# Layer 3 attention on one core: both casts of the probabilities on ScalarE, the low half of the values on VectorE

## The chip, the core and the metric

The kernel runs on one core of a Trainium2 chip (trn2). The metric is the device time of one execution in microseconds. The engines are PE (TensorE), DVE (VectorE), ACT (ScalarE), POOL (GpSimd) and SP (SyncE, which here only issues DMAs). Each has its own queue, works it off in order, and is tied to the others by semaphores alone.

## What is computed

The reference takes x (16 batches x 56 tokens x 128) through four pairs of cross attention and feed-forward, with ctx_1024 (16 x 1500 x 128) as keys and values. Layer 3's attention, the part that is changed, is plain multi-head attention with 16 heads of 8 columns, a bias on every projection and a key mask:

```python
q = (q_input @ W_Q + b_Q); k = (kv_input @ W_K + b_K); v = (kv_input @ W_V + b_V)   # 16 heads x 8
sim = jnp.einsum('bhqd,bhkd->bhqk', q, k) / jnp.sqrt(jnp.float32(D_H))
sim = jnp.where(mask, neg_inf, sim)
attn = jax.nn.softmax(sim, axis=-1)
out = jnp.einsum('bhqk,bhkd->bhqd', attn, v)
return out @ W_O + b_O
```

x then gets this sum and goes through a mixture of eight experts (`l3f`), the last stage.

## The kernel before

Layer 3's attention is `small_head_attention`: `attend_sets` (stage `l3att`) makes the outputs of all heads, `join_sets` (`l3comb`) applies W_O. The 16 heads are four sets of four. One step of `attend_sets` starts one set of one batch: 224 rows (4 heads x 56 tokens) against 1500 keys, which are 12 chunks of 125. 64 steps, batch by batch, run in a loop unrolled eight times. u is the step within the unrolled body and g = u % 4 the set. Work of three sets overlaps: in step n PE makes the scores of set n, the transposed scores of set n-1 and the output of set n-2. The loops call `one(n, u, known)` on each engine, and the order of the work is written out by hand there.

Numbers that need more than TensorE's fast format (fp32r) are split into a rounded high part and a low part, the rest. The kernel does it for queries, keys, values, maxima and probabilities. One fp32r matmul works on each part. A plain fp32 matmul is shown in the trace as two instructions of the slow kind.

PSUM has eight banks of 512 columns. Banks 0 to 2 take the scores of half a set (`rows`, 112 x 1500), bank 2 also the projection of keys for the next batch and the denominators; banks 3 to 5 the transposed scores (`turned`, two parts of six chunks), bank 5 also the projection of values; banks 6 and 7 the outputs and the transposed maxima.

The steps around the change, by engine, with the lines of the code of before:

- PE (L1949 to L2063), in this order: `values` for chunks 0 to 3 (waits for the first low part of the probabilities and for the low values); `maxima`, two transposes of the negated maxima (L2000, waits `negs_in`); `rows(0)` (L1971); `turned(0)` (L1990, waits for the copied maxima, `m_in`, and, ahead of the two chunks in bank 5, until the values in that bank have been read); `values` for chunks 4, 5 and 11; `rows(1)`; `turned(1)`; `values` for chunks 6 to 10; then the projections of keys (L1914, g < 3), denominators (L2055, g = 3) and values (L1920, all g but 1).
- ACT (L2101 to L2141): exponentials of the first part (`powers(0)`, L2110), cast of its chunks 0 to 4 into PH (`high_part`, L2116), exponentials of the second part, copy of the output (L2124), high part of the keys (L2069), high part of the values into VS (L2079), and a plain copy of the values to VF (L2081), which waits until POOL is done with VF.
- POOL (L2192 to L2209): low values VF - VS (`low_values`, L2169), block queries of the next batch (L2178), and then the low parts of the probabilities, PL = P - PH, two instructions of 5 chunks (1120 elements), each as soon as its cast is there (`ph_in`, L2208).
- DVE (L2251 to L2289): low keys (L2220), on g = 0 the reciprocal of the denominators (L2257), copy of the transposed maxima into QB (L2262), maximum of the first half of the rows (L2266), on g = 0 the division of an output (L2272), maximum of the second half (L2275), cast of the two maxima to fp32r (L2280), their low part (L2282, signals `negs_in`), and at last the cast of the second part of the probabilities (L2289, the one that POOL's second L2208 waits for).

`SPLIT` is 5: of the six chunks of each part the first five are split into PH and PL, the sixth is multiplied in fp32 (L2024). WOS holds W_O for `join_sets`; POOL clears it at the start (`cleared`), and SP fills it by eight DMAs (L1900), after the first remap of the keys and before the third context load.

In the expert stage `l3f`, POOL splits weights (L583, L585) and adds a bias (L596), while DVE works through a layer norm whose reciprocal root is made by `rsqrt`. Two of its lines:

```python
chain(v.tensor_tensor(y2, out, out, ALU.mult))     # L142
chain(v.tensor_tensor(tt, y2, half, ALU.mult))     # L143
```

Of the kernel before, what the change touches and what calls it, by code (L numbers as in the profile page):

```python
# [11 lines left out]
ALU = mybir.AluOpType  # L12
# [28 lines left out]
PART = CHUNKS // 2  # L41
SPLIT = PART - 1
HIDDEN = -2.0 ** 126
# [125 lines left out]
class Kernel(Stack):  # L169
# [1597 lines left out]
    def small_head_attention(self):  # L1767


        t = self.t  # L1770
        self.stage = "l3"
        with ExitStack() as whole:
            OC = self.sb(whole, "OC", [SETS * VCOLS, BATCH, SETS, TOK])
            cout = self.sb(whole, "cout", [128, 1])
            WOS = self.sb(whole, "WOS", [SETS * VCOLS, SETS, D])
            wos_in = self.sem(whole, "wos_in")
            self.attend_sets(OC, cout, WOS, wos_in)
            self.join_sets(OC, cout, WOS)

    def attend_sets(self, OC, cout, WOS, wos_in):  # L1780
# [10 lines left out]
        with ExitStack() as ctx:  # L1791
# [6 lines left out]
            cT = [self.sb(ctx, f"cT{s}", [128, KEYS]) for s in range(2)]  # L1798
            VF = self.sb(ctx, "VF", [CHUNK, 64, 8])
            SEL = self.sb(ctx, "SEL", [ROWS17, SETS, VCOLS])  # L1800
# [21 lines left out]
            P = [self.sb(ctx, f"P{s}", [CHUNK, CHUNKS, SET_ROWS]) for s in range(2)]  # L1822
            PH, PL = ([self.sb(ctx, f"{n}{s}", [CHUNK, 2, SPLIT, SET_ROWS], F32R) for s in range(2)]
                      for n in ("PH", "PL"))
# [5 lines left out]
                 "maskb_in"))  # L1830
            (k_ps, kh_in, kl_in, v_ps, vh_in, vf_in, vl_in, den_ps, inv_in, on_in, qb_in, sr_ps, top_in, nh_in, negs_in, t_ps, m_in,
             st_ps, p_in, ph_in, pl_in, o_ps, o_in) = (self.sem(ctx, n) for n in (
                 "k_ps", "kh_in", "kl_in", "v_ps", "vh_in", "vf_in", "vl_in", "den_ps", "inv_in", "on_in", "qb_in", "sr_ps", "top_in", "nh_in",
                 "negs_in", "t_ps", "m_in", "st_ps", "p_in", "ph_in", "pl_in", "o_ps", "o_in"))
# [11 lines left out]
            def _(sp):  # L1846
# [47 lines left out]
                for b in range(BATCH):  # L1894
                    if b == 0:
                        sp.wait_ge(cleared, 1)
                        for h in range(SETS):
                            for r in range(2):
                                at = VCOLS * h + 8 * r
                                sp.dma_start(WOS[at:at + 8, :, :], t["L3_xattn_W_O"].rearrange(  # L1900
                                    "(g h j) d -> h j g d", g=SETS, h=SETS)[h]).then_inc(wos_in, 16)
                    else:
                        extract(b - 1)
                    if b + 2 < BATCH:
                        sp.wait_ge(v_ps, BANKS * (b + 1))
# [19 lines left out]
            def _(pe):  # L1925
# [23 lines left out]
                def one(n, u, known):  # L1949
# [27 lines left out]
                    def turned(part):  # L1977
# [7 lines left out]
                        for k in range(PART):  # L1985
                            if k == 4 and part == 0 and g != 1 and (
                                    known is None or known - 1 < GROUPS - (SETS if g else 0)):
                                pe.wait_ge(vf_in, thirds)
                            at = CHUNK * (PART * part + k)
# [14 lines left out]
                    def values(chunks):  # L2004
# [11 lines left out]
                        for k in chunks:  # L2016
                            first, last = k == 0, k == CHUNKS - 2
                            if k % PART < SPLIT:
                                pe.matmul(out, VS[s][:, k, g, :], PH[u % 2][:, k // PART, k % PART, :],  # L2019
                                          start=first, stop=False)  # L2020
                                mm = pe.matmul(out, VS[s][:, k, g, :], PL[u % 2][:, k // PART, k % PART, :],  # L2021
                                               start=False, stop=last)
# [52 lines left out]
            def values_out(act, b, s, i, bank):  # L2075
# [3 lines left out]
                act.copy(heads(s, i)[:, :, 0:8], src).then_inc(vh_in, 1)  # L2079
                act.wait_ge(vl_in, b * BANKS + i)  # L2080
                act.copy(VF[:, :, :], src).then_inc(vf_in, 1)  # L2081

            @block.scalar
            def _(act):
# [16 lines left out]
                def one(n, u, known):  # L2101
# [11 lines left out]

                    def high_part():
                        act.wait_ge(p_in, 2 * n - 1)
                        act.copy(PH[s][:, 0, :, :], P[s][:, 0:SPLIT, :]).then_inc(ph_in, 1)  # L2116

# [9 lines left out]
                    if live(known, 1, GROUPS):  # L2127
                        powers(0)
                        high_part()
                        powers(1)  # L2130
                    if live(known, 2, GROUPS):
                        outputs()
# [14 lines left out]
            def _(g):  # L2147
# [5 lines left out]
                chain(g.memset(negs[:, :, :, :].bitcast(F32), 1.0))  # L2153
                chain(g.memset(WOS[:, :, :], 0.0))
                chain(g.memset(SEL[:, :, :], 0.0))
# [10 lines left out]

                def low_values(b, s, i):
                    g.wait_ge(vf_in, b * BANKS + i + 1)
                    g.tensor_tensor(heads(s, i)[:, :, 8:16], VF[:, :, :], heads(s, i)[:, :, 0:8], ALU.subtract  # L2169
                                    ).then_inc(vl_in, 1)  # L2170

                def low_queries(n):
# [9 lines left out]

                for i in range(BANKS):
                    low_values(0, 0, i)
                g.wait_ge(vl_in, BANKS)
                for n in range(2 * SETS):
                    low_queries(n)
                g.wait_ge(q3_in, 2 * SETS)
                for x in range(SETS):
                    block_queries(0, 0, x)  # L2190

                def one(n, u, known):  # L2192
                    b, x = n // SETS, u % SETS
                    if x == 3 and live(known, 1, GROUPS - SETS):
                        low_values(b + 1, 1 - u // SETS, 0)
                    if x == 0 and live(known, 1, GROUPS - SETS):
                        low_values(b, u // SETS, 1)
                    if x == 1 and (known is None or SETS < known < GROUPS):
                        low_values(b, u // SETS, 2)
                    if known is None or known < GROUPS - SETS:  # L2200
# [3 lines left out]
                    if live(known, 1, GROUPS):  # L2204
                        s = (u - 1) % 2
                        for part in range(2):
                            g.wait_ge(ph_in, 2 * n - 1 + part)
                            g.tensor_tensor(PL[s][:, part, :, :], P[s][:, PART * part:PART * part + SPLIT, :],  # L2208
                                            PH[s][:, part, :, :], ALU.subtract).then_inc(pl_in, 1)  # L2209

# [3 lines left out]
            def _(v):  # L2214
                chain = Chain(v, step)

                def low_keys(b, i, bank):
                    at = slice(BANK_KEYS * i, BANK_KEYS * i + BANK_KEYS)
                    v.wait_ge(kh_in, b * BANKS + i + 1)
                    v.scalar_tensor_tensor(out=kl[:, at], in0=PS[:, bank, 0:BANK_KEYS], scalar=bk[:, 0:1],  # L2220
                                           in1=kh[:, at], op0=ALU.add, op1=ALU.subtract).then_inc(kl_in, 1)

                layer_norm(v, chain, XN, X, ln, 1e-5, xn_ready)
# [23 lines left out]
                for n in range(2 * SETS):  # L2247
                    scaled(n)
                v.wait_ge(cleared, 1)

                def one(n, u, known):  # L2251
# [3 lines left out]
                    if g == 0 and live(known, 8, GROUPS):  # L2255
                        v.wait_ge(den_ps, (n - SETS) // SETS)
                        v.reciprocal(inv[:, :, :].rearrange("p g q -> p (g q)"), PS[0:ROWS17, 2, 0:SET_ROWS]  # L2257
                                     ).then_inc(inv_in, 1)
                    if live(known, 1, GROUPS):
                        a = (u - 1) % UNROLL  # L2260
                        v.wait_ge(t_ps, n)
                        v.tensor_copy(QB[a // SETS][96:99, a % SETS, :],  # L2262
                                      PS[0:3, 6 + a % 2, 256:256 + SET_ROWS]).then_inc(m_in, 1)
                    if live(known, 0, GROUPS):
                        v.wait_ge(sr_ps, 2 * n + 1)
# [7 lines left out]
                    if live(known, 0, GROUPS):  # L2273
# [10 lines left out]
                    if live(known, 1, GROUPS):  # L2284
                        s = (u - 1) % 2
                        v.wait_ge(p_in, 2 * n)
                        if known is None or known >= 3:
                            v.wait_ge(o_ps, n - 2)
# [3 lines left out]
                v.wait_ge(on_in, BATCH)  # L2292

# [131 lines left out]
```

## Time and profile before

| | |
|---|---|
| median of 3 runs | 1998.93 us (1997.3 to 2000.82) |
| profiled execution | 1990.49 us, its span 1988.8 us |
| granted TensorE clock over the span | 0.909 of full speed |
| PE, DVE, ACT, POOL busy | 1638.5, 1367.2, 929.6, 701.4 us |

The profile is one execution. It names each instruction by engine, line and tiles, gives its start and duration, and says for idle time which instruction ended it. An instruction that waits for a semaphore counts as idle until it starts; a wait after its start is part of its duration. Matmuls overlap, so the duration of one (0.27 us for 224 columns) is longer than the distance to the next. The loop of `l3att` runs from about 1280 to 1825 us, the experts from about 1850 us to the end.

### The profile page before, as it was taken

How to read it: one execution, taken by the hardware profiler on the slowest of the kernel's cores; microseconds unless marked ns; L12 is line 12 of the kernel's file. 1: busy time of each engine (PE TensorE's matmuls, PEld its weight loads, DVE VectorE, ACT ScalarE, POOL GpSimd, SP SyncE). 2: the span in 40 equal slices, each digit the busy share in tenths (PEclk: the TensorE clock that was granted, in tenths of full speed). 3: DMA queues.
4: the chain of work that ended last, by engine and by line, in shares of the span. 5: the costliest groups of instructions: out<-in, count | busy, mean ns of one | idle time of the engine just before them, and what ended most of it. 6: DMA issues, size and time to landing. Idle time of an engine off the chain costs nothing. (4 is left out here: it accounts for less than half of the span.)

```text
span 1988.8 us, 30871 instructions
## 1 busy us (share of the span) xinstructions
PE 1638.5 (82%) x10566; PEld 1375.8 (69%) x10566; DVE 1367.2 (69%) x2269; ACT 929.6 (47%) x1342; POOL 701.4 (35%) x607
## 2 busy tenths in 40 slices
PE   3994546433899999999999994599999999996796
PEld 2994334313789999999999972277777777774695
DVE  5214523465588888888888843578888888884498
ACT  1432211120466666666666622366666666663331
POOL 1110000000034323333332300378787878774231
PEclk8997878765799999999999997799999999998798
DMA  2113254003111111111011000424343434340110
GB/s 52 33 32 119 92 168 147 2 0 94 44 32 46 49 31 31 52 40 31 31 59 34 0 3 3 107 69 107 87 104 87 104 87 104 87 89 3 54 43 20
DMA packets 97952, 118.10 MB, mean 59 GB/s; under 512 B 16641, under 2 KB 82722, under 8 KB 97890
## 3 DMA queue, kind: packets, MB, share of 16 engines
q1 hardware_dynamic: 97890, 117.32, 22.5%
q8 instruction: 34, 0.56, 0.1%
q14 instruction: 28, 0.23, 0.0%
HBM read 78.51 MB, written 0.46 MB: 40 GB/s over the span
## 5 line engine op out<-in xcount | busy, mean ns | idle before, releaser
L2208 POOL TENSOR_TENSOR l3att_PL<-l3att_P,l3att_PH 125x1120 fp32r<-125x1120 f32 x128 | 330.1, 2579 | 122.1 <-DVE l3att_PH L2289 61.3
L1605 ACT CAST l2att_PT<-PS 125x512 fp32r<-125x512 f32 x336 | 175.5, 594 | 221.4 <-PE PS L1540 221.4
L1670 DVE TENSOR_REDUCE l2att_neg<-PS 128x1 f32<-128x1500 f32 x112 | 192.7, 1721 | 75.2 <-PE PS L1533 75.1
L2110 ACT ACTIVATE l3att_P<-PS 125x1344 f32<-125x1344 f32 x128 | 165.5, 1293 | 137.4 <-PE PS L1990 135.4
L1676 DVE TENSOR_TENSOR l2att_PT<-PS,l2att_PT 125x512 fp32r<-125x512 f32 x336 | 210.4, 681 | 2.0 <-ACT l2att_PT L1605 2.0
L1496 POOL CAST l_QH<-l_QP 128x128 fp32r (+1 forms) x112 | 54.2, 484 | 390.0 <-POOLq L1285 228.5
L1540 PEld LDWEIGHTS PS<-all_ident,l2att_P 128*125 128x125 f32 x1344 | 164.8, 189 | 14.5 <-DVE l2att_P L1684 6.0
L1614 ACT ACTIVATE l2att_P<-PS,l2att_neg 128x1500 f32<-128x1500 f32 x112 | 171.2, 1528 | 5.2 <-DVE l2att_neg L1670 5.2
L1572 PE MATMUL PS<-l2att_PT,l2att_cc 125*128 125x256 f32 x576 | 170.6, 296 | 0.0
L1540 PE MATMUL PS<-all_ident,l2att_P 128*125 128x128 f32 x1344 | 166.5, 274 | 4.5 <-DVE l2att_P L1684 4.5
L1574 PE MATMUL PS<-l2att_PT,l2att_cc 125*128 125x256 f32 x576 | 162.9, 283 | 0.0
L1576 PE MATMUL PS<-l2att_PT,l2att_cc 125*128 125x256 f32 x576 | 162.8, 283 | 0.0
L2019 PE MATMUL PS<-l3att_PH,l3att_VS 125*68 125x224 f32 x640 | 148.9, 274 | 12.9 <-POOL l3att_PL L2208 12.7
L2275 DVE TENSOR_REDUCE l3att_negm<-PS 112x1 f32<-112x1500 f32 x64 | 110.2, 1721 | 62.0 <-PE PS L1971 62.0
L2021 PE MATMUL PS<-l3att_PL,l3att_VS 125*68 125x224 f32 x640 | 144.0, 266 | 0.0
L1971 PE MATMUL PS<-l3att_KS,l3att_QB 97*112 97x500 f32 x384 | 125.0, 428 | 19.4 <-DVE l3att_inv L2257 7.7
L1531 PE MATMUL PS<-l2att_cTh,l_QH 128*128 128x500 f32 x336 | 133.4, 397 | 5.8 <-DVE l2att_cTl L1698 4.5
L1532 PE MATMUL PS<-l2att_cTl,l_QH 128*128 128x500 f32 x336 | 131.7, 392 | 0.0
L1533 PE MATMUL PS<-l2att_cTh,l_QL 128*128 128x500 f32 x336 | 131.1, 390 | 0.0
L1684 DVE TENSOR_SCALAR l2att_P<-l2att_P,l2att_inv 128x1500 f32<-128x1500 f32 x112 | 121.3, 1083 | 3.9
L2266 DVE TENSOR_REDUCE l3att_negm<-PS 112x1 f32<-112x1500 f32 x64 | 110.1, 1721 | 19.1 <-PE PS L1971 19.1
L1990 PEld LDWEIGHTS PS<-l3att_QB,l3att_KS 99*125 99x125 f32 x768 | 100.0, 190 | 23.3 <-DVE l3att_QB L2262 16.2
(510 smaller groups left out, 3755.6 us busy)
## 6 DMA issues: line engine op xcount, KB each, us to landing
l3att_KS<-l3att_kh SPq DMA_DIRECT2D x128, 187.5 KB, 4.0
l_cT<-in_ctxT SPq DMA_DIRECT2D x8, 1500.0 KB, 26.0
l_c<-in_ctx SPq DMA_DIRECT2D x8, 1500.0 KB
l_cT<-in_ctxT SPq DMA_DIRECT2D x16, 750.0 KB
l_c<-in_ctx SPq DMA_DIRECT2D x16, 750.0 KB
l3att_cT<-in_ctxT SPq DMA_DIRECT2D x16, 750.0 KB, 4.8
l3att_KS<-l3att_kl SPq DMA_DIRECT2D x64, 187.5 KB, 3.8
l0f_w<-in_L_ffn_W SPq DMA_DIRECT2D x16, 256.0 KB, 3.1
```

The lines of the kernel that those rows point to most:

```text
L1540: mm = pe.transpose(PS[0:CHUNK, 3 * s1 + g, 128 * j:128 * j + 128], P[s1][:, at:at + CHUNK], ident[:, :])
L1572: pe.matmul(out2, cc[:, slot, k, 0, :], PT[:, k, two, 0, :], start=first, stop=False)
L1574: pe.matmul(out2, cc[:, slot, k, 1, :], PT[:, k, two, 0, :], start=False, stop=False)
L1576: mm = pe.matmul(out2, cc[:, slot, k, 0, :], PT[:, k, two, 1, :], start=False, stop=last)
L1605: act.copy(PT[:, 4 * g:4 * g + 4, PLACE[u1], 0, :], PS[0:CHUNK, 3 * s1 + g, :].rearrange("k (c r) -> k c r", r=128)).then_inc(hi_in, 1)
L1614: act.activation(Pv, Pv if padded else PS[:, 3 * s:3 * s + 3, 0:BANK_KEYS], ACT.Exp, bias=neg[:, s:s + 1], accum_out=total[:, s:s + 1]).th ...
L1670: v.tensor_reduce(neg[:, s:s + 1], E, XY_AXES, ALU.max, negate=True).then_inc(top_in, 1)
L1676: v.tensor_tensor(PT[:, 4 * g:4 * g + 4, at, 1, :], PS[0:CHUNK, 3 * s1 + g, :].rearrange("k (c r) -> k c r", r=128), PT[:, 4 * g:4 * g + 4 ...
L2019: pe.matmul(out, VS[s][:, k, g, :], PH[u % 2][:, k // PART, k % PART, :], start=first, stop=False)
L2021: mm = pe.matmul(out, VS[s][:, k, g, :], PL[u % 2][:, k // PART, k % PART, :], start=False, stop=last)
L2110: act.activation(P[s][:, PART * part:PART * part + PART, :].rearrange("p (i j) r -> p i (j r)", j=2), PS[0:CHUNK, 3:6, 0:2 * SET_ROWS], AC ...
L2208: g.tensor_tensor(PL[s][:, part, :, :], P[s][:, PART * part:PART * part + SPLIT, :], PH[s][:, part, :, :], ALU.subtract).then_inc(pl_in, 1)
```

## The change

ScalarE makes both casts of the probabilities. PH and PL hold eleven chunks in a row: chunk 5 is now split as well, and only chunk 11 is left in fp32. ACT's `high_part(0)` and POOL's first subtraction cover six chunks (1344 elements), the second of each five (1120). DVE's cast L2289 is gone. The low values are made by DVE from the PSUM bank itself, behind the copy of the maxima and ahead of the first maximum of the step; ACT's copy to VF, the tile VF and POOL's subtraction are gone, and PE's wait ahead of bank 5 in `turned(0)` is on DVE's result. DVE's cast of the two maxima becomes a max of the tile with itself. The reciprocal waits for the division of the batch before. WOS lies in XN, and POOL clears it after its first block queries (`wos_clear`, for which SP waits).

```diff
-SPLIT = PART - 1
+HALVED = CHUNKS - 1
-            WOS = self.sb(whole, "WOS", [SETS * VCOLS, SETS, D])
+            WOS = self.XN[0:SETS * VCOLS, 0:SETS, :]
# PE
                             if k == 4 and part == 0 and g != 1 and (
                                     known is None or known - 1 < GROUPS - (SETS if g else 0)):
-                                pe.wait_ge(vf_in, thirds)
+                                pe.wait_ge(vl_in, thirds)
-                            if k % PART < SPLIT:
+                            if k < HALVED:
# SP
-                        sp.wait_ge(cleared, 1)
+                        sp.wait_ge(wos_clear, 1)
# ACT
                 act.copy(heads(s, i)[:, :, 0:8], src).then_inc(vh_in, 1)
-                act.wait_ge(vl_in, b * BANKS + i)
-                act.copy(VF[:, :, :], src).then_inc(vf_in, 1)
-                    def high_part():
-                        act.wait_ge(p_in, 2 * n - 1)
-                        act.copy(PH[s][:, 0, :, :], P[s][:, 0:SPLIT, :]).then_inc(ph_in, 1)
+                    def high_part(part):
+                        some = slice(PART * part, min(PART * part + PART, HALVED))
+                        act.wait_ge(p_in, 2 * n - 1 + part)
+                        act.copy(PH[s][:, some, :], P[s][:, some, :]).then_inc(ph_in, 1)
                         powers(0)
-                        high_part()
+                        high_part(0)
                         powers(1)
+                        high_part(1)
# POOL
-                chain(g.memset(WOS[:, :, :], 0.0))
-                for i in range(BANKS):
-                    low_values(0, 0, i)
-                g.wait_ge(vl_in, BANKS)
+                g.wait_ge(xt_ps, 2)
+                g.memset(WOS, 0.0).then_inc(wos_clear, 1)
-                    if x == 3 and live(known, 1, GROUPS - SETS):
-                        low_values(b + 1, 1 - u // SETS, 0)
...
-                            g.tensor_tensor(PL[s][:, part, :, :], P[s][:, PART * part:PART * part + SPLIT, :],
-                                            PH[s][:, part, :, :], ALU.subtract).then_inc(pl_in, 1)
+                            some = slice(PART * part, min(PART * part + PART, HALVED))
+                            g.tensor_tensor(PL[s][:, some, :], P[s][:, some, :], PH[s][:, some, :],
+                                            ALU.subtract).then_inc(pl_in, 1)
# DVE
+                def low_values(b, s, i, bank):
+                    v.wait_ge(vh_in, b * BANKS + i + 1)
+                    v.tensor_tensor(heads(s, i)[:, :, 8:16], PS[0:CHUNK, bank, :].rearrange("p (x j) -> p x j", j=8),
+                                    heads(s, i)[:, :, 0:8], ALU.subtract).then_inc(vl_in, 1)
                     scaled(n)
+                    if n < BANKS:
+                        low_values(0, 0, n, 3 + n)
+                v.sem_inc(on_in, 1)
                         v.wait_ge(den_ps, (n - SETS) // SETS)
+                        v.wait_ge(on_in, (n - SETS) // SETS)
                                       PS[0:3, 6 + a % 2, 256:256 + SET_ROWS]).then_inc(m_in, 1)
+                    if g == 3 and live(known, 1, GROUPS - SETS):
+                        low_values(b + 1, 1 - u // SETS, 0, 5)
+                    if g == 0 and live(known, 1, GROUPS - SETS):
+                        low_values(b, u // SETS, 1, 5)
+                    if g == 1 and (known is None or SETS < known < GROUPS):
+                        low_values(b, u // SETS, 2, 5)
-                        v.tensor_copy(negs[:, u % 2, :, 1], negm[:, u % 2, :]).then_inc(nh_in, 1)
+                        v.tensor_tensor(negs[:, u % 2, :, 1], negm[:, u % 2, :], negm[:, u % 2, :], ALU.max
+                                        ).then_inc(nh_in, 1)
-                        v.tensor_copy(PH[s][:, 1, :, :], P[s][:, PART:PART + SPLIT, :]).then_inc(ph_in, 1)
```

## Rows read from the trace of the kernel before

**Rows 1.** The page, its first part: busy time, share, instructions of each engine.
```profile
PE 1638.5 (82%) x10566; PEld 1375.8 (69%) x10566; DVE 1367.2 (69%) x2269; ACT 929.6 (47%) x1342; POOL 701.4 (35%) x607
```
**Rows 2.** Two stretches: length, then PE, PEld, DVE, ACT, POOL busy, clock, DMA, GB/s.
```profile
1340.00:1780.00 440.00, 415.39 (x2770) 322.07 (x2767) 371.23 (x386) 280.57 (x333) 351.67 (x200) 1.00 0.42 96
1802.00:1820.00 18.00, 11.81 (x84) 9.29 (x84) 12.22 (x13) 8.12 (x10) 11.43 (x5) 1.00 0.00 1
```
**Rows 3.** Timeline of one step: start, duration (us), engine, line, operation, tiles [idle before].
```profile
1361.92 2.56 POOL L2208 TENSOR_TENSOR l3att_PL<-l3att_P,l3att_PH 125x1120 fp32r<-125x1120 f32 x1 [0.20 <-ACT l3att_PH L2116]
...
1363.14 1.36 DVE L2280 CAST l3att_negs<-l3att_negm 112x2 fp32r<-112x2 f32 x1
...
1364.54 0.16 DVE L2282 TENSOR_TENSOR l3att_negs<-l3att_negm,l3att_negs 112x2 fp32r<-112x2 f32 x1
...
1364.61 0.32 PE L2019 MATMUL PS<-l3att_PH,l3att_VS 125*68 125x224 f32 x1 [0.34 <-POOL l3att_PL L2208]
...
1364.62 0.74 DVE L2289 CAST l3att_PH<-l3att_P 125x1120 fp32r<-125x1120 f32 x1
...
1365.28 0.73 DVE L2220 SCALAR_TENSOR_TENSOR l3att_kl<-PS,l3att_bk,l3att_kh 128x500 fp32r<-128x500 f32 x1
...
1365.49 0.35 PE L2000 MATMUL PS<-all_ident,l3att_negs 112*3 112x112 f32 x2
...
1366.04 0.38 DVE L2262 CAST l3att_QB<-PS 3x224 fp32r<-3x224 f32 x1
...
1366.48 0.92 PE L1990 MATMUL PS<-l3att_QB,l3att_KS 99*125 99x224 f32 x6
...
1366.59 1.72 DVE L2266 TENSOR_REDUCE l3att_negm<-PS 112x1 f32<-112x1500 f32 x1 [0.16 <-PE PS L1971]
...
1367.43 1.29 ACT L2110 ACTIVATE l3att_P<-PS 125x1344 f32<-125x1344 f32 x1 [2.44 <-PE PS L1990]
...
1368.36 0.93 PE L1971 MATMUL PS<-l3att_KS,l3att_QB 97*112 97x500 f32 x3
...
1368.75 1.13 ACT L2116 CAST l3att_PH<-l3att_P 125x1120 fp32r<-125x1120 f32 x1
...
1369.13 0.82 PE L1990 MATMUL PS<-l3att_QB,l3att_KS 99*125 99x224 f32 x6
...
1369.96 2.57 POOL L2208 TENSOR_TENSOR l3att_PL<-l3att_P,l3att_PH 125x1120 fp32r<-125x1120 f32 x1 [1.41 <-ACT l3att_PH L2116]
```
**Rows 4.** By tile negs: count, shortest/median/longest ns, first and last start (us).
```profile
L2280 DVE CAST l3att_negs<-l3att_negm x64: 170/1378/1484, 1286.0 to 1809.9; 112x2 fp32r<-112x2 f32 x64
L2282 DVE TENSOR_TENSOR l3att_negs<-l3att_negm,l3att_negs x64: 161/163/165, 1286.2 to 1811.3; 112x2 fp32r<-112x2 f32 x64
```
**Rows 5.** Timeline in the experts, POOL then DVE; last, line L142 by source.
```profile
1899.57 1.28 POOL L585 TENSOR_TENSOR l3f_w1l<-l3f_w,l3f_w1h 128x512 fp32r<-128x512 f32 x1
1900.81 2.35 POOL L596 TENSOR_TENSOR l3f_XB<-all_XN,l3f_b 128x1024 f32<-128x1024 f32 x1
...
1899.76 1.12 DVE L142 TENSOR_TENSOR l3f_nwork<-l3f_rstd 128x8 f32<-128x8 f32 x1
1900.91 2.28 DVE L143 TENSOR_TENSOR l3f_nwork<-l3f_nwork 128x8 f32<-128x8 f32 x1
...
L142 DVE TENSOR_TENSOR l3f_nwork<-l3f_rstd x27: 166/167/1116, 1852.4 to 1978.7; 128x8 f32<-128x8 f32 x27
```
**Rows 6.** Groups by line, 1340 to 1780 us: count | busy us, mean ns | idle before.
```profile
L2208 POOL TENSOR_TENSOR l3att_PL<-l3att_P,l3att_PH 125x1120 fp32r<-125x1120 f32 x107 | 276.0, 2580 | 89.1 <-DVE l3att_PH L2289 52.0 <-ACT l3att_PH L2116 37.1
...
L2169 POOL TENSOR_TENSOR l3att_VS<-l3att_VF,l3att_VS 125x512 fp32r<-125x512 f32 x40 | 50.0, 1251 | 0.0
L2024 PE MATMUL PS<-l3att_P,l3att_VS 125*68 125x224 f32 x212 | 48.7, 352 | 0.0
...
L2220 DVE SCALAR_TENSOR_TENSOR l3att_kl<-PS,l3att_bk,l3att_kh 128x500 fp32r<-128x500 f32 x40 | 29.3, 732 | 0.0
L2257 DVE RECIPROCAL l3att_inv<-PS 68x224 f32<-68x224 f32 x14 | 21.7, 1547 | 0.0
```

More of the change, by code:

```diff
@@ L1798, in attend_sets @@
             cT = [self.sb(ctx, f"cT{s}", [128, KEYS]) for s in range(2)]
-            VF = self.sb(ctx, "VF", [CHUNK, 64, 8])
             SEL = self.sb(ctx, "SEL", [ROWS17, SETS, VCOLS])
@@ L1822, in attend_sets @@
             P = [self.sb(ctx, f"P{s}", [CHUNK, CHUNKS, SET_ROWS]) for s in range(2)]
-            PH, PL = ([self.sb(ctx, f"{n}{s}", [CHUNK, 2, SPLIT, SET_ROWS], F32R) for s in range(2)]
+            PH, PL = ([self.sb(ctx, f"{n}{s}", [CHUNK, HALVED, SET_ROWS], F32R) for s in range(2)]
                       for n in ("PH", "PL"))
@@ L1830, in attend_sets @@
                  "maskb_in"))
-            (k_ps, kh_in, kl_in, v_ps, vh_in, vf_in, vl_in, den_ps, inv_in, on_in, qb_in, sr_ps, top_in, nh_in, negs_in, t_ps, m_in,
+            (k_ps, kh_in, kl_in, v_ps, vh_in, vl_in, wos_clear, den_ps, inv_in, on_in, qb_in, sr_ps, top_in, nh_in, negs_in, t_ps, m_in,
              st_ps, p_in, ph_in, pl_in, o_ps, o_in) = (self.sem(ctx, n) for n in (
-                 "k_ps", "kh_in", "kl_in", "v_ps", "vh_in", "vf_in", "vl_in", "den_ps", "inv_in", "on_in", "qb_in", "sr_ps", "top_in", "nh_in",
+                 "k_ps", "kh_in", "kl_in", "v_ps", "vh_in", "vl_in", "wos_clear", "den_ps", "inv_in", "on_in", "qb_in", "sr_ps", "top_in", "nh_in",
                  "negs_in", "t_ps", "m_in", "st_ps", "p_in", "ph_in", "pl_in", "o_ps", "o_in"))
@@ L2017, in values @@
                             first, last = k == 0, k == CHUNKS - 2
-                            if k % PART < SPLIT:
-                                pe.matmul(out, VS[s][:, k, g, :], PH[u % 2][:, k // PART, k % PART, :],
+                            if k < HALVED:
+                                pe.matmul(out, VS[s][:, k, g, :], PH[u % 2][:, k, :],
                                           start=first, stop=False)
-                                mm = pe.matmul(out, VS[s][:, k, g, :], PL[u % 2][:, k // PART, k % PART, :],
+                                mm = pe.matmul(out, VS[s][:, k, g, :], PL[u % 2][:, k, :],
                                                start=False, stop=last)
@@ L2165, in _ @@
                 g.sem_inc(cleared, 1)
[L2167 to L2170, printed above, removed]
                 def low_queries(n):
@@ L2190, in _ @@
                     block_queries(0, 0, x)
+                g.wait_ge(xt_ps, 2)
+                g.memset(WOS, 0.0).then_inc(wos_clear, 1)
                 def one(n, u, known):
                     b, x = n // SETS, u % SETS
-                    if x == 3 and live(known, 1, GROUPS - SETS):
-                        low_values(b + 1, 1 - u // SETS, 0)
[L2196 to L2199, printed above, removed]
                     if known is None or known < GROUPS - SETS:
@@ L2283, in one @@
                                         ALU.subtract).then_inc(negs_in, 1)
[L2284 to L2288, printed above, removed]
-                        v.tensor_copy(PH[s][:, 1, :, :], P[s][:, PART:PART + SPLIT, :]).then_inc(ph_in, 1)
                 run_steps(v, GROUPS, LAG, UNROLL, one, peeled=1)
-                v.wait_ge(on_in, BATCH)
+                v.wait_ge(on_in, BATCH + 1)
     def join_sets(self, OC, cout, WOS):
```

## The prediction

> **What bounds the kernel now.** The change lies in layer 3's attention alone, so I read the timings of that stage and leave the rest at its present time. The busy table [rows 1] gives PE 82% of the span and DVE 69%. The table of stretches [rows 2] says more: from 1340 to 1780 us PE is busy 415.39 of 440 us at a granted clock of 1.00, DVE 371.23, POOL 351.67, ACT 280.57. So PE is nearly full, and an edit that only lightens DVE can win little. The subtract of L2282, once a step, starts from 1286.2 to 1811.3 us [rows 4]: 63 steps take 525.1 us, 8.33 us each.
>
> The timeline of one step [rows 3] is to be read as a ring. POOL makes the low half of the probabilities (L2208, first part, "PL0") from 1361.92 to 1364.48. PE stood idle 0.34 us for it and starts the value matmuls at 1364.61 (L2019, "V4"); then come the transposes of the maxima (L2000, 1365.49), DVE's copy of them (L2262, ends 1366.42), the first transposed scores (L1990, end 1367.40), ACT's exponential (L2110, 1367.43), ACT's cast (L2116, 1368.75 to 1369.88), and PL0 again at 1369.96. That is 8.04 us round. A second ring runs beside it: reduce (L2266), rows (L1971), reduce (L2275), keys, V4, transposes, rows. They are close to each other.
>
> The third thing to see is the cast of L2280. It moves 2 elements and takes 1.36 us in that step, 1378 ns in the median and 170 ns at the least [rows 3, 4]. It starts at 1363.14 and ends at 1364.50, 0.02 us after POOL's PL0. So DVE waited for POOL's instruction. L2282, behind it, reads two SBUF tiles and takes 163 ns, but no POOL instruction ran then: the second POOL subtract (PL1) waits for DVE's own cast L2289.
>
> **Does the new max escape this wait?** The change replaces the cast by a max of `negm` with itself, and hands the cast that kept POOL quiet (L2289) to ACT. In the trace of before there is a twin of both instructions, in the expert layer's square root [rows 5]. L142 is a tensor_tensor of one tile with itself, 8 elements, and L143 a tensor_tensor of two tiles, 8 elements. Undisturbed L142 takes 0.17 us. With POOL's L585 running (to 1900.85) it takes 1.12 us and ends at 1900.88. POOL's next instruction L596 starts at once, and L143, issued at 1900.91, takes 2.28 us and ends at 1903.19, 0.03 us after L596. So a tensor_tensor with both inputs in SBUF waits as the cast does, and between two dependent DVE instructions POOL's queued instruction gets in.
> The Trainium skill has a rule against this change: "SBUF — State Buffer", section "SBUF: two separate sides", says that a DVE instruction with two SBUF inputs and a GpSimd instruction that reads SBUF exclude each other for a whole instruction. [rows 5] agree. The page "VectorE: DVE Perf Modes", section "Why `tensor_tensor` can't do 2×_2P or 4×", taken alone, would let the fp32 max keep clear of the two-port mode and so of the wait, which would give the second rival's time below; [rows 5] speak against that reading.
>
> **The new step, term by term.** Let H0 and H1 be ACT's casts, P0 and P1 its exponentials, P0 starting at 0.
> H0 starts at 1.32 [rows 3]. It grows from 1120 to 1344 elements: 1.13 by proportion is 1.36, by the slope between cast and exponential (1.29 - 1.13 for 224 elements) 1.29; I take 1.33. It ends at 2.65. PL0 starts 0.08 later, as in [rows 3]. Its slope is (2580 - 1251) / (1120 - 512) = 2.19 ns per element [rows 6], so 1344 elements take 3.07: it ends at 5.80.
> P1 starts when the second half of the transposed scores is there: 1.77 from DVE's first reduce to PE's rows (L1971), 0.77 to L1990, 0.82 for it [rows 3]; that reduce starts some 0.45 ahead of P0, right behind the low values, so P1 starts at about 2.9. Then 1.29 and 1.13: H1 ends at about 5.4, before PL0. So PL1 stands ready and follows PL0 at once, 2.56 more (5 chunks, as now), to 8.36.
> DVE's second reduce follows the rows (0.93) and ends at -0.45 + 1.77 + 0.97 + 1.72 = 4.0, so the max waits 1.8 us for PL0 and ends at 5.83; the subtract waits for PL1 and ends at 8.39.
> Behind the subtract, on DVE, stand the low keys, the copy of the maxima and now the low values, and PE's transposed scores wait for both of the latter. From the subtract's end: low keys 0.66 (0.73 less the overlap of 0.07 with the instruction ahead, 1365.36 to 1365.28), copy 0.41, low values 0.66, then the last two matmuls of L1990 with the hops on either side 0.48 (0.39 of the 0.92 for six, 0.06 and 0.03) = 2.21. The transposes need 0.44 from the subtract to the copy and hide behind the low keys. The low values read a bank and one SBUF tile like L2220, whose 732 ns for 500 elements [rows 6] I take for 512; that kind overlapped PL1 undisturbed at 0.73 [rows 3]. The same subtraction on POOL takes 1.25 (L2169), the upper bound; 0.68 for 512 contiguous elements is about the lower.
> One turn: 8.39 + 2.21 = 10.60. Where no low values are made (one step in four) 1.01 follows the copy directly (1366.42 to 1367.43): 8.39 + 0.66 + 0.41 + 1.01 = 10.47. Where the reciprocal (1.55, [rows 6]) stands for the low keys: 11.42. Four steps: 2 x 10.60 + 10.47 + 11.42 = 43.09, 10.77 a step. The last three have neither low keys nor low values: 8.39 + 0.84 (transposes 0.36, copy 0.38, hops 0.10) + 1.01 = 10.24.
> 60 x 10.77 + 3 x 10.24 = 676.9, less 525.1 = +151.8. At the end PL1 no longer waits for DVE's last cast: -0.6.
>
> **What is at nothing.** The eleventh split chunk replaces one fp32 chunk (two L2024 of 352 ns, [rows 6]) by two matmuls like L2019, at most 0.32 each [rows 3]: PE gains 0.06 to 0.2 a step, but it lies under DVE's 1.72 us reduce. ACT loses the copy to VF and gains H1, and POOL loses 1.25 in three of four steps; both have room (ACT about 6.4 of 10.8). The wait on `on_in` ahead of the reciprocal is a batch old. WOS is now cleared behind POOL's first block queries; SP waits for that ahead of its eight DMAs (L1900), and behind them stand the third context load and the second batch's remap, which waits for low keys made only in the first steps of the loop anyway. The start-up on POOL gets shorter by up to 3 us; I take 0 and keep -3 to +3.
>
> Sum: +151.2 us. The profiled execution took 1990.49 (span 1988.8), the median is 1998.93; 1990.49 becomes 2141.7 and the median 2150.1: **2150 us**.
>
> **Rivals.**
> 1. One wait only: H1 comes too late for PL1 to be queued, the subtract slips in behind the max. The margin is 5.80 - 5.4 = 0.4 us, which is thin. Then the first ring decides: PL0's end, 0.13, V4 0.88, transposes and copy 0.78, low values 0.66, 0.48, P0 to PL0's end 5.80 = 8.73; without low values 8.60; with the reciprocal 9.07; four steps 35.13, against 33.3. 60 x 8.78 + 3 x 8.60 - 525.1 - 0.6 = +27: 2026 us.
> 2. The max and subtract don't wait at all (the fp32 rule above): the same ring, since PL0 has grown by 0.49 and H0 by 0.20 and PE already stood waiting for PL0 in [rows 3]. About 2024. Either way slower, for the same reason.
> 3. Faster: DVE's queue is what bounds, and PL0 lands in time for V4. DVE would lose 1.21 (cast) and 0.74 (L2289) and gain 0.55 a step, and PE's idle would go: (440 - 415.39) / 53 steps = 0.46 a step [rows 2], with 0.2 of the split chunk 0.66, x 63 = -42 at the most: 1957. It decides from the point at which H0 and PL0 together are over before PE reaches V4; they are already 0.34 late in [rows 3] and grow by 0.69.
> 4. The forecast, and TensorE's clock falls besides. Of four steps PE would be busy 0.944 x 33.3 - 0.8 = 30.6 of 43.1 us, 71%. For it: no stretch of this stage was so thin for long. Against: from 1802 to 1820 it was busy 11.81 of 18 us, 66%, at 1.00 [rows 2]. If a fifth of the steps ran at 1.2 GHz, PE's 7.7 us a step would be some 15: 12 x 4 = +48, 2200.
>
> **Chances.** Forecast 0.74, one wait or none (1 and 2) 0.13, clock 0.08, faster or no change (3) 0.05. The forecast's own bounds: low values at 1.25, 0.52 x 45 = +23; hops and overlaps, some eight a turn, read from one step, 0.4 a turn either way, 25. With half of case 4 and a margin below, since the 0.4 us of rival 1 can fail in some steps only: 2100 to 2205. This kernel's timing tells changes from about 0.2%, 4 us. Faster 0.04, same 0.02, slower 0.94.
>
> **What would show it.** In the changed profile the max of L2280's place should take about 1.7 to 1.9 us and the subtract of L2282's about 2.5, ending within 0.05 of POOL's two subtracts, which follow each other without a gap. Reduce to reduce should be 10.5 to 11.4. DVE's idle should stay small, PE's idle should move to the transposes, waiting for `negs`. If the subtract takes 0.16 and PE waits for L2208 ahead of V4, rival 1 or 2 holds, and the duration of the max tells which. A clock under 1.00 between 1340 and 1900 us would be rival 4.

## The result

The changed kernel takes 2123.78 us (median of 4 runs, 2119.01 to 2130.65), the kernel before 1999.47 us: the ratio is 1.0625, 95% interval 1.059 to 1.0661. The profiled execution took 2119.01 us with a span of 2117.3. The forecast was 2150, its range 2100 to 2205.

The page of the changed kernel, its busy table, answers to [rows 1]:

```profile
span 2117.3 us, 30746 instructions
...
PE 1696.6 (80%) x10566; PEld 1414.1 (67%) x10566; DVE 1450.6 (69%) x2253; ACT 983.9 (46%) x1358; POOL 671.1 (32%) x559
```

DVE has 16 instructions fewer and is busy 83 us longer. Where that sits is in the instructions that touch the tile `negs`, the answer to [rows 4] (count, shortest, median and longest ns, first and last start; below, who waited for the subtract):

```profile
L2282 DVE TENSOR_TENSOR l3att_negs<-l3att_negm x64: 161/1934/2146, 1290.1 to 1934.3; 112x2 fp32r<-112x2 f32 x64
L2285 DVE TENSOR_TENSOR l3att_negs<-l3att_negm,l3att_negs x64: 161/2480/2495, 1290.3 to 1936.4; 112x2 fp32r<-112x2 f32 x64
...
who waited for it (us, times):
  PE PS L1999: 50.7, 34
```

The max takes 1934 ns in the median, the subtract behind it 2480; each handles two elements per partition and takes 0.16 us undisturbed. The subtract starts from 1290.3 to 1936.4 us: 63 steps in 646.1 us, 121.0 more than in [rows 4]. The two profiled executions are 128.5 us apart; of the other 7.5, 4.1 lie ahead of the first subtract and 3.4 behind the last.

But PE waited for the subtract 34 times, not 63. The timeline of two steps that follow each other, in the answer to [rows 3], shows both kinds (start, duration, engine, line; in brackets the idle time ahead):

```profile
1503.75 5.56 POOL L2195 TENSOR_TENSOR l3att_PL<-l3att_P,l3att_PH 125x1344 fp32r<-125x1344 f32 x2 [2.91 <-ACT l3att_PH L2114]
...
1504.86 1.94 DVE L2282 TENSOR_TENSOR l3att_negs<-l3att_negm 112x2 fp32r<-112x2 f32 x1
...
1505.08 1.13 ACT L2114 CAST l3att_PH<-l3att_P 125x1120 fp32r<-125x1120 f32 x1
...
1506.84 2.49 DVE L2285 TENSOR_TENSOR l3att_negs<-l3att_negm,l3att_negs 112x2 fp32r<-112x2 f32 x1
1506.91 0.32 PE L2018 MATMUL PS<-l3att_PH,l3att_VS 125*68 125x224 f32 x1 [0.93 <-POOL l3att_PL L2195]
...
1509.47 0.35 PE L1999 MATMUL PS<-all_ident,l3att_negs 112*3 112x112 f32 x2 [1.52 <-DVE l3att_negs L2285]
...
1512.58 1.59 PE L1970 MATMUL PS<-l3att_KS,l3att_QB 97*112 97x500 f32 x3
...
1513.97 1.24 PE L1989 MATMUL PS<-l3att_QB,l3att_KS 99*125 99x224 f32 x6
...
1514.17 3.07 POOL L2195 TENSOR_TENSOR l3att_PL<-l3att_P,l3att_PH 125x1344 fp32r<-125x1344 f32 x1 [4.34 <-ACT l3att_PH L2114]
...
1515.97 1.29 DVE L2282 TENSOR_TENSOR l3att_negs<-l3att_negm 112x2 fp32r<-112x2 f32 x1
...
1516.57 1.13 ACT L2114 CAST l3att_PH<-l3att_P 125x1120 fp32r<-125x1120 f32 x1
...
1517.29 0.16 DVE L2285 TENSOR_TENSOR l3att_negs<-l3att_negm,l3att_negs 112x2 fp32r<-112x2 f32 x1
...
1517.78 2.60 POOL L2195 TENSOR_TENSOR l3att_PL<-l3att_P,l3att_PH 125x1120 fp32r<-125x1120 f32 x1 [0.54 <-ACT l3att_PH L2114]
```

In the first step the second cast ends at 1506.21, before POOL's first subtraction (1503.75 + 3.07 = 1506.82). POOL's two subtractions run as one block to 1509.31 (the row with x2). The max ends with the first of them, at 1506.80, and the subtract ends with the block, at 1509.33. PE stood still for 0.93 and 1.52 us. In the second step PE is slow: the rows take 1.59 us where they took 0.93, the second transposed scores 1.24 against 0.82 [rows 3]. So ACT's second cast ends at 1517.70, 0.46 after the first subtraction, POOL's second subtraction isn't running yet, and the subtract passes in 0.16 us. The slow PE accounts for all of it: from the start of the rows to the end of the second transposed scores it is 1.57 us in the first step and 2.63 in the second, 1.06 more, and the second cast, counted from the start of the exponential, ends 1.06 us later (6.24 against 5.18).

The two steps as stretches (from reduce to reduce; length, then PE, PEld, DVE, ACT, POOL busy, granted clock, DMA, GB/s), against [rows 2]:

```profile
1500.38:1510.81 10.43, 7.43 (x45) 5.16 (x45) 8.89 (x8) 5.85 (x6) 6.54 (x4) 1.00 0.06 9
1510.81:1520.34 9.53, 9.53 (x58) 7.58 (x56) 6.62 (x7) 6.36 (x7) 5.63 (x3) 0.82 0.30 97
```

The long step has a clock of 1.00 and leaves PE idle for 3 of 10.43 us. The next has 0.82: the granted clock is 0.50 (1.2 GHz) from 1512 to 1514 us and 1.00 again from 1515. PE is busy all through, and the step is 0.9 us shorter. From step 11 on (counted from 0, at 1397.5 us) long and short steps alternate to the end. The long ones are in turn one without low values, like the one shown, and one with the reciprocal and low values (11.49 us, also at 1.00, PE busy for 8.54).

### The profile page after: what moved, and what is told of

It is laid out like the page before. It is cut to its first block and busy times, and to the rows that moved or that the text cites. A ratio compares the mean times of both kernels' runs of the same rounds, so it can differ in the third digit from the quotient of the medians.

```text
span 2117.3 us, 30746 instructions
## 1 busy us (share of the span) xinstructions
PE 1696.6 (80%) x10566; PEld 1414.1 (67%) x10566; DVE 1450.6 (69%) x2253; ACT 983.9 (46%) x1358; POOL 671.1 (32%) x559
## 5 line engine op out<-in xcount | busy, mean ns | idle before, releaser
L2195 POOL TENSOR_TENSOR l3att_PL<-l3att_P,l3att_PH 125x1344 fp32r<-125x1344 f32 (+1 forms) x128 | 359.1, 2818 | 272.6 <-ACT l3att_PH L2114 271.7
L2018 PE MATMUL PS<-l3att_PH,l3att_VS 125*68 125x224 f32 x704 | 168.2, 281 | 27.7 <-POOL l3att_PL L2195 25.6
L2277 DVE TENSOR_REDUCE l3att_negm<-PS 112x1 f32<-112x1500 f32 x64 | 110.1, 1721 | 85.6 <-PE PS L1970 85.6
L1970 PE MATMUL PS<-l3att_KS,l3att_QB 97*112 97x500 f32 x384 | 148.1, 492 | 23.9 <-DVE l3att_negm L2268 14.1
L2020 PE MATMUL PS<-l3att_PL,l3att_VS 125*68 125x224 f32 x704 | 164.8, 275 | 0.0
L2114 ACT CAST l3att_PH<-l3att_P 125x1344 fp32r<-125x1344 f32 (+1 forms) x128 | 156.2, 1220 | 4.0
L1989 PEld LDWEIGHTS PS<-l3att_QB,l3att_KS 99*125 99x125 f32 x768 | 119.0, 214 | 34.1 <-DVE l3att_QB L2258 13.2
L1989 PE MATMUL PS<-l3att_QB,l3att_KS 99*125 99x224 f32 x768 | 133.7, 305 | 2.4 <-DVE l3att_QB L2258 1.3
L2018 PEld LDWEIGHTS PS<-l3att_PH,l3att_VS 125*68 125x68 f32 x704 | 101.6, 144 | 45.0 <-issue 43.9
```

The lines of the kernel that those rows point to most:

```text
L1989: mm = pe.matmul(PS[0:CHUNK, 3 + k // 2, SET_ROWS * (k % 2):SET_ROWS * (k % 2) + SET_ROWS], KS[s][:, g, at:at + CHUNK], QB[s][:, g, :], st ...
L2018: pe.matmul(out, VS[s][:, k, g, :], PH[u % 2][:, k, :], start=first, stop=False)
L2020: mm = pe.matmul(out, VS[s][:, k, g, :], PL[u % 2][:, k, :], start=False, stop=last)
L2195: g.tensor_tensor(PL[s][:, some, :], P[s][:, some, :], PH[s][:, some, :], ALU.subtract).then_inc(pl_in, 1)
```

## The experiments

Four kernels are the changed one with an edit, run together.

**The cast again.** Is it the tensor_tensor?

```diff
-                        v.tensor_tensor(negs[:, u % 2, :, 1], negm[:, u % 2, :], negm[:, u % 2, :], ALU.max
-                                        ).then_inc(nh_in, 1)
+                        v.tensor_copy(negs[:, u % 2, :, 1], negm[:, u % 2, :]).then_inc(nh_in, 1)
```

> The changed kernel with the max of the maxima tile with itself put back to the cast of before. Theory (any DVE instruction that needs the second way into SBUF waits for POOL's whole subtraction): the cast waits as the max does, 1.9 us, the subtract behind it 2.5 us in about half the steps; 2124 us, within 8. Rival (a tensor_tensor is worse than a cast, or better): a difference of more than 0.5% from the changed kernel.

Measured: 2119.96 us, ratio to the kernel before 1.0609 (1.0591 to 1.0627), which overlaps the changed kernel's. The cast's median is 1936 ns, the subtract's 2474, and PE waits for the subtract 34 times. Max and cast are the same to this kernel.

**Three reduces.** The high part, its negative and the low part are each made by an instruction with one SBUF input. `negm` gets a fourth axis, the value and its negated high part (its shape and the index in the two reduces of the rows, also edited, are not shown).

```diff
-                        v.tensor_tensor(negs[:, u % 2, :, 1], negm[:, u % 2, :], negm[:, u % 2, :], ALU.max
-                                        ).then_inc(nh_in, 1)
+                        v.tensor_reduce(negs[:, u % 2, :, 1], negm[:, u % 2, :, 0:1], X_AXIS, ALU.max)
+                        v.tensor_reduce(negm[:, u % 2, :, 1].bitcast(F32R), negm[:, u % 2, :, 0:1], X_AXIS, ALU.max,
+                                        negate=True).then_inc(nh_in, 1)
                         v.wait_ge(nh_in, n + 1)
-                        v.tensor_tensor(negs[:, u % 2, :, 2], negm[:, u % 2, :], negs[:, u % 2, :, 1],
-                                        ALU.subtract).then_inc(negs_in, 1)
+                        with nc.allow_low_precision(reason="two terms"):
+                            v.tensor_reduce(negs[:, u % 2, :, 2], negm[:, u % 2, :, :], X_AXIS, ALU.add
+                                            ).then_inc(negs_in, 1)
```

> The changed kernel, but the high part, its negative and the low part of the maxima are made by three tensor_reduce over SBUF, each with one input. Theory (the two waits of DVE on POOL's subtractions are the loss): none of the three takes over 0.25 us, PE never waits for the low part, and the ring over POOL's first subtraction decides at 8.73 us a step: 2026 us, 2015 to 2045. Rival (the low values on DVE or the longer cast and subtraction on their own are the loss): above 2080 us. Second rival (a reduce from SBUF waits as well): 1.9 us for the first reduce and about 2124 us.

Measured: 2032.67 us, ratio 1.0171 (1.0154 to 1.0188). The tile `negs` and one step's timeline:

```profile
L2282 DVE TENSOR_REDUCE l3att_negs<-l3att_negm x64: 156/156/157, 1292.9 to 1852.0; 112x2 fp32r<-112x2 f32 x64
L2287 DVE TENSOR_REDUCE l3att_negs<-l3att_negm x64: 156/158/160, 1293.2 to 1852.3; 112x2 fp32r<-112x4 f32 x64
```
```profile
1505.41 5.61 POOL L2195 TENSOR_TENSOR l3att_PL<-l3att_P,l3att_PH 125x1344 fp32r<-125x1344 f32 x2 [2.79 <-ACT l3att_PH L2114]
...
1506.55 0.16 DVE L2282 TENSOR_REDUCE l3att_negs<-l3att_negm 112x2 fp32r<-112x2 f32 x1
1506.62 0.14 DVE L2283 TENSOR_REDUCE l3att_negm<-l3att_negm 112x2 fp32r<-112x2 f32 x1
...
1506.80 0.16 DVE L2287 TENSOR_REDUCE l3att_negs<-l3att_negm 112x2 fp32r<-112x4 f32 x1
```

All three run in the middle of POOL's block, and none is longer than 0.16 us in any of 64 steps. That takes 91 us away (2123.8 - 2032.7). A step is 559.1 / 63 = 8.87 us. By kind, from reduce to reduce, it is 8.9 us with low values, 8.5 without and 8.84 with the reciprocal (forecast for this case 8.73, 8.60 and 9.07).

**The second cast back on DVE.** One part of the change undone; the max and the subtract stay.

```diff
                         powers(1)
-                        high_part(1)
# DVE, behind the subtract of the maxima
+                    if live(known, 1, GROUPS):
+                        s = (u - 1) % 2
+                        v.wait_ge(p_in, 2 * n)
+                        if known is None or known >= 3:
+                            v.wait_ge(o_ps, n - 2)
+                        v.tensor_copy(PH[s][:, PART:HALVED, :], P[s][:, PART:HALVED, :]).then_inc(ph_in, 1)
```

> The changed kernel with one part undone: the cast of the second part of the probabilities is DVE's last instruction of the step again. Then POOL's second subtraction can't be queued behind the first. Theory: the max still waits 1.8 us, the subtract takes 0.16 in every step, the clock stays at 1.00, and a step takes 8.8 to 9.0 us: 2030 to 2050 us. Rival (the time is lost to the max's wait, not to the subtract's): above 2090 us.

Measured: 2052.13 us, ratio 1.0271 (1.0254 to 1.0288), 2 us above the stated range.

```profile
L2281 DVE TENSOR_TENSOR l3att_negs<-l3att_negm x64: 161/1943/2130, 1292.1 to 1869.3; 112x2 fp32r<-112x2 f32 x64
L2284 DVE TENSOR_TENSOR l3att_negs<-l3att_negm,l3att_negs x64: 160/162/165, 1292.3 to 1871.4; 112x2 fp32r<-112x2 f32 x64
```

The max takes 1.94 us as in the changed kernel, the subtract never waits, and the clock from 1400 to 1800 us is 1.00. So it is the second wait that costs: with the first alone the kernel is 72 us faster. The first wait is mostly hidden, because PE waits for the same POOL instruction. A step without low values takes 8.50 us here and 8.50 with the reduces, so there the wait costs nothing. The others are 0.1 to 0.3 us longer than with the reduces, and those with the reciprocal 1.0 us; how much of this is the wait and how much DVE's cast, which is back, was not separated. Both together are 19 us.

**PE filled.** Twelve matmuls whose results are thrown away, in front of the transposes.

```diff
+                    if known is None or 2 <= known < GROUPS:
+                        pe.wait_ge(top_in, 2 * n)
+                        for k in range(12):
+                            pe.matmul(PS[0:SETS * VCOLS, k % 2, 0:SET_ROWS], VS[(u - 2) % UNROLL // SETS][:, k % 4, (u - 2) % SETS, :],
+                                      PH[u % 2][:, k % 4, :], start=True, stop=True)
                     if live(known, 1, GROUPS):
                         maxima()
```

> The changed kernel with twelve more matmuls a step on PE (results thrown away) between the value matmuls of chunks 0 to 3 and the transposes, where PE idles for the low part of the maxima. Theory (a step with both waits idles PE, the granted clock falls to half in the next step, PE's second scores and with them ACT's second cast come late, the subtract slips in, and that step is the shorter one): the clock stays at 1.00, the subtract waits in nearly every step, and the kernel gets slower although its TensorE is faster: 2145 to 2170 us. Rival (the clock falls are only a cost): faster than the changed kernel, under 2115 us.

Measured: 2157.87 us, ratio 1.0808 (1.0789 to 1.0828). The tile `negs`, then the stretch from 1400 to 1800 us (length; PE, PEld, DVE, ACT, POOL busy; clock):

```profile
L2290 DVE TENSOR_TENSOR l3att_negs<-l3att_negm,l3att_negs x64: 161/2516/2528, 1290.2 to 1972.5; 112x2 fp32r<-112x2 f32 x64
...
  PE PS L1999: 18.1, 60
```
```profile
1400.00:1800.00 400.00, 352.04 (x2362) 270.71 (x2360) 353.14 (x259) 225.52 (x240) 225.25 (x112) 1.00 0.33 76
```

The clock holds at 1.00, and PE waits for the subtract 60 times instead of 34, for 0.3 us each, since the filling takes up the rest. In these steps the filling ends before the subtract does, so it adds nothing: with the reciprocal they take 11.51 us, and 11.48 in the changed kernel. The kernel with the faster TensorE is 34 us slower than the changed one. So the slow spells did open the gap through which the subtract slips. The forecast, made for a clock of 1.00, was 2150 for this case.

**What is left once the waits are gone.** The kernel with the reduces is still 34 us above the kernel before. Two terms were separated; both kernels that follow keep the three reduces.

Ten split chunks instead of eleven, so that the first cast and the first subtraction have 1120 elements (PE multiplies chunk 5 in fp32 again):

```diff
-                            if k < HALVED:
+                            if k < HALVED and k != PART - 1:
# the same line in ACT's cast and in POOL's subtraction
-                        some = slice(PART * part, min(PART * part + PART, HALVED))
+                        some = slice(PART * part, PART * part + PART - 1)
```

> The three reduces, with chunk 5 in fp32 again, so that ACT's first cast and POOL's first subtraction have 1120 elements as before. Theory (without the waits on POOL the ring over POOL's first subtraction decides, and its length counts in full): the step falls from 8.85 us by 0.49 + 0.19 = 0.68 to 8.17, or less where PE becomes the bound: 1990 us, 1984 to 2000. Rival (the kernel with the reduces is bound by something else, such as DVE's low values): above 2015 us.

Measured: 1998.75 us, ratio 1.0011 (0.9998 to 1.0023): 34 us less than with eleven. The sum of the terms, 0.68 x 63, is 43; the next run shows what stands in the way of the rest.

The first subtraction in two instructions, chunks 0 to 3 and 4 to 5:

```diff
-                        for part in range(2):
-                            g.wait_ge(ph_in, 2 * n - 1 + part)
-                            some = slice(PART * part, min(PART * part + PART, HALVED))
+                        for part, first, last in ((0, 0, 4), (0, 4, PART), (1, PART, HALVED)):
+                            if first != 4:
+                                g.wait_ge(ph_in, 2 * n - 1 + part)
+                            some = slice(first, last)
# PE
-                        parts = 1 if chunks[0] < PART else 2
-                        pe.wait_ge(pl_in, 2 * n - 4 + parts)
-                        if parts == 1:
+                        parts = {0: 1, 4: 2, 6: 3}[chunks[0]]
+                        pe.wait_ge(pl_in, 3 * n - 6 + parts)
+                        if parts < 3:
```

> The three reduces and eleven split chunks, but POOL's first subtraction is two instructions, chunks 0 to 3 and 4 to 5, and PE's value matmuls of chunks 0 to 3 wait for the first alone. Theory: the low part of chunks 0 to 3 is there 1.0 us earlier, the ring over POOL's subtraction falls to 7.8 to 7.9, and the ring of rows and reduces with PE's work decides at about 8.0 us a step: 1980 us, 1970 to 1990, faster than the kernel before. Rival (the value matmuls don't wait for that instruction but for the cast or for a free buffer): no better than the kernel with the reduces alone, 2033 us.

Measured: 1997.58 us, ratio 0.9996 (0.9987 to 1.0006). The theory's first half held, since PE stopped waiting for POOL; its 1980 was missed by 17 us. The rival's 2033 did not come either. The timeline of that kernel shows what came next:

```profile
1503.42 0.92 PE L1970 MATMUL PS<-l3att_KS,l3att_QB 97*112 97x500 f32 x3
1503.68 0.38 DVE L2259 CAST l3att_QB<-PS 3x224 fp32r<-3x224 f32 x1
1504.10 0.69 DVE L2213 TENSOR_TENSOR l3att_VS<-PS,l3att_VS 125x512 fp32r<-125x512 f32 x1
...
1504.71 1.71 DVE L2269 TENSOR_REDUCE l3att_negm<-PS 112x1 f32<-112x1500 f32 x1
```

The rows end at 1504.34, but the reduce starts at 1504.71: DVE is still at the low values. The sum priced these on the way to the exponential; here they hold up the reduce. The kernel with ten chunks has the same steps as this one (8.57 us with low values, 8.00 without, 8.25 with the reciprocal), so the low values bound it too, and the longer cast and subtraction may be worth more than the 34 us.

**The low values alone.** In the kernel before, DVE makes them from the bank; nothing else is changed.

```diff
-                act.wait_ge(vl_in, b * BANKS + i)
-                act.copy(VF[:, :, :], src).then_inc(vf_in, 1)
# POOL's low_values and its calls taken out; on DVE:
+                    if g == 3 and live(known, 1, GROUPS - SETS):
+                        low_values(b + 1, 1 - u // SETS, 0, 5)
...
```

> The kernel before with one part of the change alone: DVE makes the low parts of the values from the bank, ACT's copy and POOL's subtraction of them are gone. Theory: 0.69 us more on DVE in three of four steps, of which 0.1 to 0.2 us end up on the path: 2003 to 2010 us. Rival (a lighter POOL and ACT gain more than DVE loses): below 1994 us.

Measured: 2013.13 us, ratio 1.0077 (1.006 to 1.0094), 3 us above the stated range. 14.4 us over some 45 steps that have them is 0.32 a step, more than the 0.1 to 0.2 expected. The part on its own is a loss.

**And the other way round.** The kernel with the reduces and the subtraction in two, with the low values on POOL again:

```diff
+            VF = XN[0:CHUNK, 4:8, :].rearrange("p t (x j) -> p (t x) j", j=8)
# ACT
+                act.wait_ge(vl_in, b * BANKS + i)
+                act.copy(VF, src).then_inc(vf_in, 1)
# POOL: low_values and its calls as in the kernel before; taken out on DVE
# PE: waits for vf_in ahead of bank 5, as in the kernel before
```

> The kernel with the three reduces and POOL's first subtraction in two, and besides the low values made by POOL from ACT's copy again (the tile VF lies in XN beside WOS). Theory: on DVE the low values stood between the copy of the maxima and the first reduce and held the ring of rows and reduces up by 0.35 us in three of four steps; without them PE's work alone decides, 8.0 us a step: 1980 us, 1972 to 1988, faster than the kernel before. Rival (POOL, now with 7.5 us of work a step, or ACT gets late): 1990 us or more.

Measured: 1986.44 us, ratio 0.9937 (0.9923 to 0.995), inside the stated range. That is 11 us less than with the low values on DVE, and 12 us less than the kernel before: the fastest version of the study. A step takes (1805.4 - 1294.5) / 63 = 8.11 us, by the row of the low part in the tile `negs`:

```profile
L2298 DVE TENSOR_REDUCE l3att_negs<-l3att_negm x64: 156/158/161, 1294.5 to 1805.4; 112x2 fp32r<-112x4 f32 x64
```
Its stretch from 1400 to 1750 us (columns as above):
```profile
1400.00:1750.00 350.00, 328.32 (x2249) 258.17 (x2248) 233.85 (x315) 278.41 (x314) 311.20 (x205) 1.00 0.43 99
```

**The reduces in the kernel before.** What did the cast's 1.2 us cost there? The edit is the one of the reduces above.

> The kernel before with its cast and subtract of the maxima replaced by the three reduces. Theory (in the kernel before the cast's wait was hidden, since PE and DVE's second cast of the probabilities wait for the same POOL subtraction): the reduces take 0.16 us each and the time moves by -0.2 to 0 us a step, 1985 to 2000 us. Rival (the 1.2 us that the cast lost were on the path): below 1960 us.

Measured: 1994.92 us, ratio 0.9975 (0.9962 to 0.9988). 0.25%, as expected: the long cast of [rows 4] lay beside a wait that PE had anyway.

## Why the prediction held, and where it didn't

- **The twin in the expert layer [rows 5] was the right witness.** The max waits for POOL's first subtraction and the subtract for the second. The sizes: max 1.94 (forecast 1.8), subtract 2.49 (2.56), POOL's first subtraction 3.07 (3.07), ACT's first cast 1.32 (1.33), low values 0.69 (0.73). The Trainium skill ("SBUF — State Buffer", section "SBUF: two separate sides") says that a DVE instruction with two SBUF inputs and a GpSimd instruction that reads SBUF exclude each other for a whole instruction. The trace agrees for the max (1934 ns in the median) and the subtract (2474 to 2480 ns); the cast of the run above takes as long as the max (1936 ns). The reduces, with one SBUF input, keep clear of POOL: at most 160 ns in all 64 steps.
- **The step.** The step of 10.43 us shown above makes no low values, and the sum had 10.47 for it; with the reciprocal it takes 11.49 us, the sum had 11.42. For both waits and low values the sum had 10.60. In the filled kernel, where nearly all steps have both waits, this kind takes 10.7 us, and four steps come to 43.4 us against 43.09.
- **The term that was mis-sized is the number of such steps.** I let every step have both waits: 676.9 us. PE waited for the subtract in 34 of 64; of the others the first two take 9.7 us and the 28 behind them mostly 9.5: 646.1 us in all, 31 less. With the clock held at 1.00 the kernel comes to 2157.87, 8 from the forecast.
- **Luck.** Two misses cancelled in part. That 28 steps escaped the second wait made the kernel faster than forecast, and that the same steps ran with a slow PE gave some of it back: 9.5 us where the kernel with the reduces takes 8.9, some 17 us by that estimate. The forecast had neither.
- **Rival 1 (the subtract slips in) happened in half the steps.** Its margin of 0.4 us was named, 0.61 is what the full-speed step shows (1506.82 - 1506.21). What used it up was the slower PE. Its price was wrong for these steps, since it was made with PE at full speed (8.73) and they take 9.53.
- **Rival 4 (the clock falls) had the wrong sign.** I expected 2200 because PE's work would double. The fall came, but in short spells, and each let the subtract of its own step pass. I weighed the two rivals one by one; they were one mechanism.
- **Rival 2 (no wait at all)** is the kernel with the reduces: 2032.67 against 2024.
- **Rival 3 (faster)** fell to the two waits first. The reason stated, the longer way over the first cast and subtraction, is worth 34 us between eleven and ten chunks, and even without both the kernel is at 1998.75, not at 1957.
- **The low values** were costed at 0.13 us a step (10.60 against 10.47), on the way to the exponential. The place where they cost more is DVE's reduce: 0.32 a step in the kernel before.
- **What stood at nothing** (the eleventh chunk on PE, the clearing of WOS, the ACT copy) can't be told apart in these runs and was not tried by itself. So the 34 us between eleven and ten chunks hold PE's share of the chunk as well.

The balance: +124 us is 91 for the two waits, which the reduces take away, and 34 that go with the eleventh split chunk. The low values cost 14 us in the kernel before and 11 on top of the reduces, but don't show in that sum, because another step became shorter. From reduce to reduce, the kernel before takes 8.24 us where the low values will come, 7.9 to 8.0 where they won't, and 8.73 with the reciprocal; with the reduces and ten chunks it is 8.57, 8.00 and 8.25. A batch has two of the first kind and one of each other: 0.66 and some 0.05 us more, 0.48 less. The kernel before with the reduces alone takes 8.45 us with the reciprocal, so 0.28 of the 0.48 come with the reduces; the other 0.20 come with the rest of the change, in which DVE's second cast no longer stands ahead of the reciprocal. That this cast is the cause was not tried by itself.

## What to carry to other kernels

Before a DVE instruction is moved or replaced to avoid a wait on GpSimd, look in the trace for one with the same kinds of inputs beside a GpSimd instruction: two dependent DVE instructions can lose a whole GpSimd instruction each, and the second loss appears only when GpSimd's next instruction no longer waits for DVE. Handing a helper's input to another engine can take away the very wait that kept the helper quiet at the right time. And a long wait in the table costs only what the engines behind it wouldn't have waited for anyway: in the kernel before, taking away 1.2 us a step was worth 0.25%.

## What the runs showed of the hardware that was not expected

- The granted clock can lock to the loop: 10.43 us at 1.00 with PE idle for 3.0 us, then 9.53 us at 0.82 with PE busy throughout, in turn, from step 11 to the end (every other long step has the reciprocal and takes 11.49). Filling the idle time kept it at 1.00 from 1400 to 1800 us. What makes it fall is not shown: the step from 1336.33 to 1346.51 us, with both waits, left PE idle for 3.0 us as well, and the next one kept 1.00.
- A faster TensorE made the kernel slower (2157.87 against 2123.78 us), because, with ACT's second cast ready earlier, POOL's second subtraction got ahead of DVE's subtract in 60 steps instead of 34.
- tensor_reduce over two or four elements in SBUF takes 0.14 to 0.16 us beside a running GpSimd subtraction, where a cast of the same size took up to 2.05 and a tensor_tensor up to 2.5. The run with the reduces was made on this expectation; the prediction did not have it.
